# Local attention of a two-image block: the row maxima one step earlier, their turns where they were, spreading and projection one step later

## The reference

```python
padded = jnp.pad(feat, ((0, 0), (3, 3), (3, 3), (0, 0)), mode='edge')
patches = jnp.stack([padded[:, dy:dy + 56, dx:dx + 56, :] for dy in range(7) for dx in range(7)], axis=3)
patches = patches.reshape(2, 3136, 49, 128)
q = _lin(Q, wq_w[2], wq_b[2]).reshape(2, 3136, 8, 16)
k = _lin(patches, wk_w[2], wk_b[2]).reshape(2, 3136, 49, 8, 16)
v = _lin(patches, wv_w[2], wv_b[2]).reshape(2, 3136, 49, 8, 16)
attn = jax.nn.softmax(jnp.einsum('bnhd,bnwhd->bnhw', q, k) * scale, axis=-1)
y_win = jnp.einsum('bnhw,bnwhd->bnhd', attn, v).reshape(2, 3136, 128)
y_win = _lin(y_win, pj_w[2], pj_b[2])
...
y = g[..., 0:1] * y_cmp + g[..., 1:2] * y_sel + g[..., 2:3] * y_win + Q
```

## Time and profile before

| | us |
|---|---|
| timed runs, median of 3 | 842.41 (840.88 to 844.82) |
| the profiled execution | 849.34 |
| its span, first to last instruction | 847.5 |
| ten jobs of window attention, 433.87 to 596.88 | 163.01 |
| TensorE busy in these | 148.68 |
| VectorE busy in these | 117.44 |

### The profile page before, as it was taken

The page is one execution under the profiler, slowest core; times in us unless marked ns, Lnnn a source line. Parts: engine busy times, 40 slices in busy tenths (PEclk is TensorE's granted clock), DMA queues, the critical chain, the costliest instruction groups (busy, mean ns, idle before and its releaser), DMA issues.

```text
span 847.5 us, 14128 instructions
## 1 busy us (share of the span) xinstructions
PE 718.2 (85%) x5053; PEld 374.7 (44%) x5053; DVE 623.4 (74%) x1260; ACT 354.4 (42%) x609; POOL 201.4 (24%) x323
## 2 busy tenths in 40 slices
PE   4937966877489999997899899999988999999993
PEld 2525532333134444444455555555534545455551
DVE  6976445555677999996767767777729889999960
ACT  2160224434423344341445454454561351546566
POOL 1010122323324444440610010010056046600000
PEclk9966798999867999997799999999999999999998
DMA  5000055555588000001455665665100000000000
GB/s 223 0 1 0 19 141 126 143 145 135 139 201 220 1 0 1 2 0 56 124 147 142 164 172 135 173 165 150 37 4 1 0 0 1 1 19 20 38 39 38
DMA packets 52519, 66.22 MB, mean 78 GB/s; under 512 B 10590, under 2 KB 48226, under 8 KB 50594
## 3 DMA queue, kind: packets, MB, share of 16 engines
q1 hardware_dynamic: 49282, 43.08, 19.0%
q10 hardware_dynamic: 3168, 22.24, 9.5%
HBM read 43.03 MB, written 21.57 MB: 76 GB/s over the span
## 4 chain that ended last, share of the span: by engine, by line
PE 40%; DVE 20%; issue 5%; DMA 5%; ACT 4%; SPq 0%; POOL 0%; ACTq 0%; DVEq 0%
PE banks L870 12%; PE banks L810 5%; PE banks L794 5%; PE banks L772 4%; DVE mx L1241 4%; DVE sm L1254 3%; DMA Q<-nT 3%; PE banks L825 3%; DVE AC L1073 2%; DVE wn L1298 2%; DVE sm L1256 2%; DVE X L1326 2%; DMA FP<-nT 1%; PE banks L711 1%; PE banks L756 1%
## 5 line engine op out<-in xcount | busy, mean ns | idle before, releaser
L972 ACT ACTIVATE P<-banks 126x480 f32<-126x480 f32 (+2 forms) x196 | 100.2, 521 | 126.4 <-PE banks L794 102.3
L1298 DVE TENSOR_REDUCE wn<-banks 128x4 f32<-128x728 f32 x112 | 102.0, 914 | 40.6 <-PE banks L772 39.5
L870 PE MATMUL banks<-FP,PTB 128*128 128x392 f32 x384 | 129.5, 493 | 2.1 <-DVE c L1329 1.2
L1073 DVE SCALAR_TENSOR_TENSOR AC<-XT,vec,AC 128x1540 f32<-128x1540 f32 (+5 forms) x48 | 117.9, 2461 | 1.1
L870 PEld LDWEIGHTS banks<-FP,PTB 128*128 128x128 f32 x384 | 72.7, 190 | 56.8 <-DVE FP L1367 2.1
L501 POOL TENSOR_TENSOR SEB<-SEB,rg 112x392 f32<-112x392 f32 x112 | 58.3, 541 | 90.2 <-DVE rg L1261 90.1
L485 POOL TENSOR_TENSOR pk<-pr,pk 128x434 bf16<-128x434 f32 (+1 forms) x42 | 42.7, 1018 | 136.7 <-DVE pk L1181 136.7
L810 PE MATMUL banks<-P,Vw 126*17 126x120 f32 (+2 forms) x1568 | 74.3, 263 | 0.0
L1170 DVE TENSOR_TENSOR pr<-pf,pk 128x434 f32<-128x434 f32 (+1 forms) x42 | 31.9, 760 | 57.1 <-ACT pk L927 56.6
L951 ACT ACTIVATE SEB<-SEB 112x424 f32<-112x424 f32 x56 | 31.2, 557 | 89.8 <-DVE SEB L1244 89.8
L731 PE MATMUL banks<-PTB,VP 106*128 106x448 f32 x112 | 54.2, 572 | 5.1 <-ACT PTB L960 5.1
(11 more groups left out here) (228 smaller groups left out, 1255.3 us busy)
## 6 DMA issues: line engine op xcount, KB each, us to landing
k_parts<-pk SPq DMA_DIRECT2D x84, 108.5 KB, 2.8
Vw<-v_rows SPq DMA_DIRECT2D x84, 66.9 KB
q_parts<-pk SPq DMA_DIRECT2D x42, 112.0 KB, 2.7
K<-k_parts ACTq DMA_DIRECT2D x7, 651.0 KB, 6.0
v_rows<-vst SPq DMA_DIRECT2D x14, 263.5 KB
X<-in_x SPq DMA_DIRECT2D x2, 1568.0 KB, 8.1
out_y<-zs SPq DMA_DIRECT2D x8, 392.0 KB, 2.3
K<-k_parts ACTq DMA_DIRECT2D x7, 434.0 KB, 3.6
```

Of the source, the lines that this page charges most:

```text
L870: last = mm(bank(2 + place_in_unit, C, ZPIX), WT[:, dy, part, C * grp:C * (grp + 1)], D[:, part, QROWS * q + dy:QROWS * (q + 1) + dy, :].r ...
L972: a(P[q % 4][0:BKEYS[b], 0:4 * BQ[b]], PS[0:BKEYS[b], 4 + q % 2, 0:4 * BQ[b]], ACT.Exp).then_inc(sem("w_exp"), 1)
L1073: return ve.scalar_tensor_tensor(out=o, in0=src(ro + dy, rn, co + dx, cn), scalar=v(wcol + t), in1=o, op0=ALU.mult, op1=ALU.add)
L1298: ve.tensor_reduce(dst, src, AX.X, ALU.max, negate=True).then_inc(sem("w_slot_read"), 1)
```

## The change

All of A moves one step earlier against the scores (`LEAD` 13 instead of 12). `TURN_AT` is counted from the same start, and one more there leaves S where it was. D and Y move one step later. Sums, reciprocals and parts stay.

```diff
-        LEAD = 12
+        LEAD = 13
         BUFS = 3
         PVLAG = 3
         AHEAD = VRING - PVLAG
         LOADS = 16 * 2 * len(TRUNS)
         MAX_AT = (0, 1, 3, 5, 7, 8, 10, 12)
-        TURN_AT = (4, 8, 11, 15)
+        TURN_AT = (5, 9, 12, 16)
         TILE_NEEDED = {0: 0, 2: 1, 6: 2, 8: 3}
-        SUMS_AT, RECIP_AT, PARTS_AT, NORM_AT, Y_AT = 17, 21, 22, 27, 30
+        SUMS_AT, RECIP_AT, PARTS_AT, NORM_AT, Y_AT = 17, 21, 22, 28, 31
         STEP_RANGE = range(-LEAD, STEPS - STEPJ + Y_AT + 1)
```

## The result

| | before | changed |
|---|---|---|
| median of the timed runs, us | 844.21 (840.88 to 848.6, 20 runs) | 840.59 (833.51 to 846.87, 20 runs) |
| ratio, with its interval | | 0.994 (0.9912 to 0.9967) |
| the profiled execution, us | 849.34 | 840.68 |
| its span | 847.5 | 838.9 |

A forecast was written before the change was run, and what follows sets the result against it. TensorE was taken to set the pace, idle 1.43 us a job in two waits. Eleven jobs at 1.0 us less, minus 0.5 at the start, give 10.5: 842.4 to 831.9 us, range 827.5 to 841, forecast's own 829 to 834.

The forecast's parts named there:

- 837 to 842: Rival: D waits for the reciprocals' transfer; landing in 5.0 us gives 842, 4.4 gives 837; half gain 0.15, none 0.12.
- 839 to 842: Rival, nothing but a shift: A1's wait and VectorE's lateness after Y's addition leave 0 to 0.3 us a job; no gain 0.12.
- The steady walk: Steady jobs, walked from D's end: S's 0.85 and the scores' 0.48 us waits vanish; a job takes 15.3 us against 16.30.
- A1's new wait: TensorE before A1, which wants the bank pair that D had: a new wait of 0.5 us a job.
- D's margin: D in step 0 needs the reciprocals' transfer, taken to land in 3.9 us: 0.1 us of waiting a job.
- Restarts and scraps: TensorE's restarts of the empty pipeline and scraps in a steady job: some 0.3 us a job.
- Tile 1's turn: Rival: SP sends this turn after ACT's load, landing 2.1 us late; each job gains 1.0, loses 2.1: 854 us; chance 0.10.
- Eleven jobs: The eleven jobs whose Y has A behind it: 1.0 us less in each, 11.0 us in all.
- At the start ... I count 0.5 lost: First job: S2's copy falls behind A7's reduction, 0.9 us later, its transfer behind the 1152 KB load: 0.5 us lost.

The follow-up runs named there:

- dy_late: The kernel before with D and Y one step later and GpSimd's eight weight-building operations moved from the first job to the last: 838.36 us, ratio 0.9909.
- after_late: The changed kernel with GpSimd's eight weight-building operations moved from the first job to the last: 834.58 us, ratio 0.9892 to before.
- s0_later: The changed kernel with the turn S0 one step later (TURN_AT 6 instead of 5): 840.18 us, ratio 0.9914 to before.
- before_late: The kernel before with GpSimd's eight weight-building operations moved from the first job to the last: 843.38 us, ratio 0.9994.
- lead_only: The kernel before with only the A one step earlier (LEAD 13, TURN_AT one more), D and Y as before: 840.53 us, ratio 0.9941.
- after_fourth: The changed kernel run once more, unaltered, for a profile: 839.16 us, one run.

## Why the prediction was right or wrong

The direction was right, and so was the mechanism in the steady jobs. The size was wrong: 10.5 us were counted, and 3.6 (medians) to 5.2 (pooled) came. The profiles give 6.2, and the stretches above account for the 4.3 that are missing there; what lies between the 6.2 and the medians is within the scatter of single executions. That 840.6 lies inside the range up to 841, and in the span of two rivals (837 to 842, 839 to 842), is chance: neither rival's mechanism is what happened.

- **The steady walk held.** S3 ahead of Y: S's 0.84 us and the scores' 0.48 us a job are gone. A job is 15.50 us where 15.3 was walked.
- **A1's new wait:** 0.5 forecast, 0.39 measured, at the place named.
- **D's margin:** 0.1 counted for the reciprocals. In the ten jobs of the changed kernel D never waited for RB; the transfers landed 3.3 to 3.5 us after their issue, and not 3.9 or 5.0. That rival (837 to 842) did not happen, though the time falls in its span.
- **Restarts and scraps, 0.3 a job, were too small.** 15.50 - 14.42 - 0.39 leaves 0.7. With A1's and D's terms this makes 1.1 of idle and scraps against 0.9 counted: 2 us over ten jobs. The rows don't name its parts; that it is the restarts behind each A and S is my reading of them.
- **Tile 1's turn** (the rival of the other sign): sent at 507.42 with 0.48 us of lead over the load, it landed 1.84 us later. It did not fall behind, in any of the four profiles: the lead was 0.19 to 0.83 us wherever a load follows, the landing 1.8 to 2.0 us. The rule that an increment lands only after earlier writes of the same DMA engine (the Trainium skill, "DMA: Bandwidth & Descriptors", section "Queues, rings and completion order") was not put to the test there. In the first jobs of `dy_late` and `after_late` turns behind a load took 5.1 and 5.3 us, as in the earlier trace rows. `s0_later` shows how thin the margin is: at a lead of 0.04 and 0.08 us the landing took 5.74 and 5.19. Which write came first on a DMA engine no trace here shows. The rival was right on the price of a late turn, and the change came within 0.2 us of it.
- **Eleven jobs** gave 8.1 + 1.4 = 9.5 us of the 11.0; the 1.5 that lack are the scraps above, on the whole.
- **The step that failed is "At the start ... I count 0.5 lost".** By the same windows it is 3.9 - 0.8 = 3.1. Its parts are 1.0 of work that only changed sides of the border, 1.1 of waiting, and 1.8 of TensorE at half the clock, less 0.8. So the true loss is 2.1 us, four times what I counted; the border's 1.0 is missing from the eleventh job on, where 1.2 us came by the windows and 0.2 without the shift, against 1 counted. I priced the start by its transfers and by A7's reduction and took every operation's duration from the steady jobs. But GpSimd, idle in the argument, builds weights during that very job, and VectorE's splits last up to 1.8 us there instead of 0.17. `after_late` gave 3.9 us of the stretch back. The trace of before showed held splits already, twice, at no cost that the timed runs can tell (`before_late`: 0.9994). The second thing that I put at nothing is the clock: the prediction names its fall as a danger for the ten jobs only, where it stayed at 1.00, while in the first stretch of before it was at 0.82. That the waits behind held splits bring its fall on is what the order in time suggests; it isn't shown, as `lead_only` has such a wait without a fall.
- **What I had not seen at all:** moving A one step ahead is redundant once Y is moved, for it frees S3 of the same pair. It adds the start's loss and some 0.2 us a job; D and Y alone are at 0.9855 and 0.99 in two measurements, medians of 833.11 and 836.59, 4.0 to 7.5 us under the change's 840.6.

The changed kernel's gain is thus what D and Y alone earn (8 to 12 us by their two ratios) less what its `LEAD` costs: 3.5 - 0.8 at the start (37.3 against 33.8 from the first scores on, 9.35 against 10.2 before them) and 1.7 in the ten jobs (155.1 against 153.4). `LEAD` 13 pays nothing here with Y at 31.

## What to carry to other kernels

When a change moves several things at once, walk each of them alone: here one number (`Y_AT`) carried the whole gain, and another (`LEAD`) gave about half of it back. The steady state and the start need walks of their own, and in the start the durations must be read from the start's own rows, next to what every other engine does at that moment, and with the granted clock of that stretch. A transfer that must stay ahead of another queue's load needs a lead that survives some scatter; here 0.2 us still did, and 0.08 did not. Two items that share a pair of banks strictly in turn should be placed by who must wait for whose reader: a cheap item with a long chain behind it goes ahead of the long one.

## What the runs showed of the hardware

**VectorE behind GpSimd.** A tensor-tensor operation of 8 elements a row took 1.66 to 1.74 us beside a GpSimd operation of 1.80 to 1.82, and 0.17 us without one. With GpSimd's work moved, all of the first job's were short, and some were held at the new place instead (1.02 and 1.72 us in `dy_late`, 1.61 in `before_late`). The Trainium skill, "SBUF — State Buffer", section "SBUF: two separate sides", calls the port pair shared by the two engines an exclusive lock, held for a whole instruction; on VectorE's side it is taken by an operation in a 2-port mode, and by one with two SBUF inputs when the GpSimd operation reads SBUF. The trace agrees: L1306 reads `wn` and `wnb`, both in SBUF, and at 407.06 it ends with GpSimd's L525 (408.79 and 408.76). The cast L1304 has one input and was held as well, for 1.79 us at 414.43; in which mode it ran the trace doesn't say.

**The granted clock inside a busy stretch.** Windows of `s0_later` in its steady jobs:

```profile
500.00:546.30 46.30, 42.01 (x711) 23.90 (x709) 35.33 (x77) 22.31 (x45) 4.19 (x18) 1.00 0.63 168
546.30:553.10 6.80, 6.61 (x50) 3.26 (x50) 1.48 (x5) 1.59 (x4) 0.00 (x0) 0.50 0.47 143
```

The clock stood at half, 1.2 GHz, for 6.8 us, and again for 3.4 us from 566.8. In the 46 us before the first fall TensorE was busy for 42.01, but the fall isn't in the midst of busy time: it begins at 546.3, inside the wait of 2.61 us that ends at 546.49 (the line is shown above), and the second one 0.4 us behind a wait of 2.02 that ends at 566.42. Behind shorter waits it happened too: `after_fourth` falls for 3.4 us at 611.0 and `after_late` at 607.1, both 0.2 us behind a wait of 0.83. Between the first scores and the first Y each fall, of before too, begins inside a wait of 1.2 to 2.2 us or at most 1.9 us behind its end. Most waits of such a length bring none: the other three profiles of the changed kernel have the same 0.83 us ahead of the last job's Y and keep the clock, and `lead_only` keeps it through 2.20 and 2.42. So in these profiles the clock falls behind single waits of 0.8 to 2.6 us, but not behind each, and what decides stays open. The waits of the steady jobs of before, 0.85 us each, brought no fall in three profiles. Over 74 timed runs of before the time goes with the mean granted clock (correlation -0.74), and the two kernels' mean clocks, 0.932 and 0.930, hardly differ.
